# Moving one pair's query preparation from slot 8 to slot 3 of a 16-slot schedule

## Chip, core and metric

One Trainium2 chip, one core used, everything in float32 (some tiles in its rounded matmul form, some small ones in bf16). The metric is device time of one call in microseconds, median of the runs shown. The engines are PE (matmul), DVE (VectorE), ACT (ScalarE), POOL (GpSimd) and SP (SyncE, which here only issues DMAs).

## What is computed

Three layers over x (32 batches of 64 tokens, 256 wide), cut to what matters here:

```python
x = x + xattn(layernorm(x), ctx)     # 16 heads of 16; ctx is (32, 1601, 256)
#   q = qdq(x) @ qdq(wq).T + bq;  k, v = split(ctx @ wkv.T + bkv)
#   o = softmax(q k^T / 4) v;     out = qdq(o) @ qdq(wp).T + bp
x = x + scan(layernorm(x))           # x_proj, softplus(dt), selective scan over 64 tokens
x = x + moe(layernorm(x))            # 64 experts, top 8, capacity 2*2048*8/64
```

`qdq` divides a row by its largest absolute value over 127, rounds, clips and multiplies back. The change touches only where the queries q are made and how the values v are dealt over time. All of it lies in the first phase, which does attention, scan and routing; expert and combine phases follow it.

## The kernel before

**Pairs, slots and strips.** Two batches (128 tokens) are a pair, i; there are 16. A pair has 16 slots, one for each strip of scores: batch b (strips 0 to 7 are b=0, 8 to 15 are b=1), half g of the heads, two heads s. Step G is pair G // 16, slot G % 16. All engines walk over G, each with its own hand-written order and semaphores between them; an engine never passes a waiting instruction.

In step G, PE does in this order: scores of strip G (`scores`, 12 matmuls into the one score area S, four PSUM banks), the turning of the probabilities of strip G-1 (13 transposes in four jobs `turn(G, 0..3)`, called T0 to T3 below), one unit of the values of a batch (`v_mm`), the products of earlier probabilities with values (`times_v`), and the keys of strip G+4 (`k_mm`). Small jobs of the rest of the layers stand in between as `MIX` says: (slot, place) to names. Scores of G wait for the exponential of G-1, which reads S.

DVE takes the row maximum of S (`strip_max`), copies values out (`v_up`), does the mixer's elementwise work (`rest_a`, `rest_b`, `rest_c`, `scan_unit`, `sum_unit`), makes the low part of the keys (`k_low`), and then what stands at the slot's end. ACT does the exponential (`soft`), the copies of the four turned jobs (`turned`), the high part of the keys (`k_up`).

**The ring.** T, V, K jobs and all small ones write into a ring of three PSUM banks W, by the job's number mod 3 in the list that `jobs_at` makes. A job waits on PE (`take`) until the job three before it has been copied out: by ACT if that was a T job, by DVE for every other.

```python
    if G % SLOTS in NO_VALUES:
        return turns + small_at(G, 0) + keys + small_at(G, 1)
    return turns[:2] + small_at(G, 0) + v + turns[2:] + small_at(G, 1) + keys + small_at(G, 2)
```

In a slot of `NO_VALUES` there is no V job; all four T jobs come first. There ACT's order is T0, T1, T2, exponential, T3, keys' high part; elsewhere it is T0, T1, exponential, T2, T3, keys.

**The queries.** For pair i+1 the kernel loads its x (SP, L430), then on DVE `moments_q` (L889 to L891), `norm_q` (L933, L872 to L874) and `round_q` (L883 to L885), each at the end of one slot behind `k_low`; then PE turns the result (job XQ, L579), DVE copies it (`x_up`, L943), PE multiplies with wq (job Q, L588), DVE adds the bias (`q_out`, L951). POOL takes the reciprocal root between `moments_q` and `norm_q` (L485) and parts the queries into high and low (`part_q`, L495 to L499); SP deals them to the four row groups (L398) in slot 12 for b=0 and slot 0 of the next pair for b=1.

**The values.** A batch has 13 tiles of keys in seven units: six of two tiles, and unit 5, the last tile alone (68 keys). Units are made in the order 0 to 6, one a slot.

The mixer of a pair runs behind it: its steps m are slot 4 of the next pair (m=0) to slot 3 of the one after (m=15). In slots 0 to 3 of pair i it is pair i-2 that is finished (scan's last unit in slot 0, third norm in 1, logits in 2, top 8 and places in 3). In slots 4 to 8 it is pair i-1 (quantised attention output, projection, second norm, x_proj, dt).

Of the kernel before, what the change touches and what calls it, by code (L numbers as in the profile page):

```python
# [20 lines left out]
PAIRS = TOK // P  # L21
# [13 lines left out]
V_UNITS = [[2 * u, 2 * u + 1] for u in range(KT // 2 - 1)] + [[KT - 1], [KT - 3, KT - 2]]  # L35
BANKS = 3
WIDTHS = [4, 3, 3, 3]
NO_VALUES = (0, 8)
ALL_STRIPS = PAIRS * SLOTS
CLEARS = 2 * SLOTS  # L40
Y_CLEARS = 16
# [12 lines left out]
END = SLOTS * (PAIRS + 1) + LAG  # L54

MIX = {(4, 0): ["O3"], (5, 0): ["oqT"], (5, 1): ["proj"], (6, 0): ["ln2T"], (6, 1): ["xp"], (7, 0): ["dt"],
       (8, 0): ["XQ"], (8, 1): ["Q"], (10, 0): ["O0"], (14, 0): ["O1"], (1, 0): ["yT"],
       (2, 0): ["O2", "ln3T"], (2, 1): ["logits"], (3, 2): ["pos"]}

QS = NS // 4  # L60
UNITS = 2 * NS // QS
# [24 lines left out]
def values_at(G):  # L86

    i, slot = divmod(G, SLOTS)
    if 1 <= slot <= 7 and i < PAIRS:
        return i, 1, slot - 1  # L90
    if slot >= 9 and i + 1 < PAIRS:
        return i + 1, 0, slot - 9
    return None
# [115 lines left out]
def mixer_phase(nc, io, dram):  # L209
    with ExitStack() as ctx:  # L210
# [78 lines left out]
        ln3T = oqT  # L289
# [86 lines left out]
        def _(sp):  # L376
# [39 lines left out]
            for G in range(END):  # L416
                i, slot = divmod(G, SLOTS)
                cur, nxt = i < PAIRS, i + 1 < PAIRS
                p, m = mixer_at(G)
                if slot == 0 and cur:  # L420
                    deal_queries(i, 1)
                if slot == 12 and nxt:
                    deal_queries(i + 1, 0)
                if G < CLEARS:
                    clear(G)
                elif G < CLEARS + Y_CLEARS:
                    clear_y(G - CLEARS)
                if slot == 0 and nxt:
                    sp.wait_ge(ring_full, full_at("XQ", i))
                    sp.dma_start(x_q[:], x_rows(i + 1)).then_inc(x_in, 16)  # L430
                if slot == 3 and 1 <= i <= PAIRS:
                    after(sp, dve_up, dve_at(i - 2, "X2"))
                    sp.dma_start(x_res[:], x_rows(i - 1)).then_inc(xr_in, 16)
                if nxt and slot in (4, 11):
                    sp.wait_ge(ring_full, full_at("K", G + STRIPS - (1 if slot == 4 else 0)))
                    load_ctx(i + 1, slot // 8)
                if m == 2 and p is not None:
                    sp.wait_ge(ring_free["dve"], free_at("xp", p))
                    sp.dma_start(dram["bc"], BCT[:]).then_inc(bc_out, 16)

                    sp.wait_ge(bc_out, 16 * (p + 1))
                    for part, landed in enumerate((b_in, c_in)):
                        own = slice(part * NS, (part + 1) * NS)
                        sp.dma_start(BC[:, own, :].rearrange("p n t -> p (n t)"),
                                     dram["bc"][own, :].rearrange("n t -> (n t)").partition_broadcast(P)).then_inc(landed, 16)
                if m == 13 and p is not None:
                    sp.wait_ge(dve_up, dve_at(p, "LN3"))
                    sp.dma_start(dram["x3"][bass.ds(p * P, P), :], x3[:]).then_inc(x3_out, 16)
# [6 lines left out]
        def _(pool):  # L455
# [72 lines left out]

            for i in range(PAIRS + 2):
                ended, prev, nxt = i >= 2, 1 <= i <= PAIRS, i + 1 < PAIRS  # L530
                if ended:
                    pool.wait_ge(dve_up, dve_at(i - 2, "V3"))
                    pool.tensor_tensor(st[:, 17:18], st[:, 16:17], neg_half[:], ALU.pow).then_inc(pool_up, 1)  # L533
                if nxt:
                    rstd_q(i + 1)
                if prev:
                    pool.wait_ge(dve_up, dve_at(i - 1, "V2"))
                    pool.tensor_tensor(st[:, 9:10], st[:, 8:9], neg_half[:], ALU.pow).then_inc(pool_up, 1)  # L538
                if prev:
                    for unit in range(UNITS // 2):  # L540
                        scan_input(i - 1, unit)
                if nxt:
                    part_q(i + 1)
                for part in range(4):
                    if ended and i != PAIRS:
                        scatter(i - 2, part)
                    if prev:
                        scan_input(i - 1, UNITS // 2 + part)
                if i == PAIRS:
                    for part in range(4):  # L550
                        scatter(i - 2, part)
# [317 lines left out]
        def _(dve):  # L869
# [303 lines left out]
            for G in range(END):  # L1173
# [8 lines left out]
                for job in small_at(G, 0):  # L1182
                    if job[0] == "O":
                        norm_o(job[1])
                if slot == 8 and nxt:
                    x_up(i + 1)
                if mix and m < 15:
                    rest_a(p, m, link)
# [13 lines left out]
                    route_link = route_begin(i - 2)  # L1202
                if G + STRIPS < ALL_STRIPS:
                    k_low(G + STRIPS)
                if slot == 8 and nxt:
                    q_out(i + 1)
                if mix:
                    if m - FIRST_DECAY - 1 in SUMMED_LATE:
                        sum_unit(p, m - FIRST_DECAY - 1, link)
                    rest_c(p, m, link)  # L1210
                if slot == 1 and nxt:
                    q_link = moments_q(i + 1)
                if slot == 2 and nxt:
                    norm_q(i + 1, q_link)
                if slot == 4 and nxt:
                    round_q(q_link)
                if mix and m == 15:
                    link.end()
# [398 lines left out]
```

## Time and profile before

| | |
|---|---|
| median of 3 runs | 2306.09 us (2305.89 to 2307.5) |
| profiled execution | 2303.75 us, span 2302.0 us |
| PE busy | 2101.8 us (91%) |
| DVE busy | 1752.8 us (76%) |
| ACT busy | 1444.5 us (63%) |
| POOL busy | 677.5 us (29%) |

PE's ends are modelled and its matmuls are pipelined, so rows on PE can overlap and its share says little about free time. The start of a row is what to go by. The 256 steps of the first phase reach from about 34 us to 1770 us. A step is best measured from the first score matmul of one strip to that of the next.

### The profile page before, as it was taken

What the parts mean: (1) busy time and instruction counts of PE and PEld (TensorE: products, weight loads), DVE (VectorE), ACT (ScalarE), POOL (GpSimd) and SP (SyncE); (2) the same over time, 40 slices, a digit from 0 to 9 for tenths busy, and PEclk for the clock granted to TensorE, in tenths of its full rate; (3) what the DMA queues carried; (4) which work ended last, traced back from release to release, by engine and by line L of the source; (5) the groups of instructions that cost most, each with busy time, mean ns of one, the idle gap of its engine ahead of it and who ended that gap; (6) DMA issues with size and microseconds to landing.
All of it is one profiled execution on the core that took longest, in us unless ns stands there. A gap on an engine that the chain in (4) does not pass through costs nothing. (4 is left out here: it accounts for less than half of the span.)

```text
span 2302.0 us, 56038 instructions
## 1 busy us (share of the span) xinstructions
PE 2101.8 (91%) x21448; PEld 1454.3 (63%) x21448; DVE 1752.8 (76%) x3728; ACT 1444.5 (63%) x3012; POOL 677.5 (29%) x646
## 2 busy tenths in 40 slices
PE   7999999999999999999999999999997149999975
PEld 5666666666666666666666666666665037777754
DVE  5557887979797878888888888887978736656646
ACT  2667676868676767676767767676767124445433
POOL 1002040404031322213130404040403437777770
PEclk9999999999999999999999999999999569999998
DMA  7585662323131313232323233232320136676648
GB/s 225 195 283 208 235 256 70 113 81 89 72 88 72 93 67 93 74 86 77 88 84 101 88 72 105 55 105 56 109 51 32 54 119 211 198 232 209 202 137 329
DMA packets 132711, 294.16 MB, mean 128 GB/s; under 512 B 21899, under 2 KB 89143, under 8 KB 126304
## 3 DMA queue, kind: packets, MB, share of 16 engines
q1 hardware_dynamic: 114016, 255.89, 35.2%
q0 software_dynamic: 18432, 34.69, 4.3%
q8 instruction: 174, 2.85, 0.5%
q14 instruction: 89, 0.73, 0.1%
HBM read 165.40 MB, written 108.27 MB: 119 GB/s over the span
## 5 line engine op out<-in xcount | busy, mean ns | idle before, releaser
L799 ACT ACTIVATE sb_probs<-S,sb_negmax 128x1604 f32<-128x1604 f32 x256 | 409.4, 1599 | 246.7 <-DVE sb_negmax L977 246.3
L791 ACT ACTIVATE sb_probsT<-W 128x384 f32<-128x384 f32 (+1 forms) x1024 | 473.9, 513 | 66.3 <-PE W L637 63.6
L637 PE MATMUL W<-sb_ident,sb_probs 128*128 128x128 f32 (+1 forms) x3328 | 484.1, 280 | 23.3 <-DVE sb_o_tok L990 11.9
L977 DVE TENSOR_REDUCE sb_negmax<-S 128x1 f32<-128x1604 f32 x256 | 465.8, 1820 | 2.4 <-PE S L627 1.2
L637 PEld LDWEIGHTS W<-sb_ident,sb_probs 128*128 128x128 f32 (+1 forms) x3328 | 363.0, 139 | 148.4 <-issue 68.5
L610 PE MATMUL W<-sb_wkv_in,sb_ctx 128*128 128x256 f32 (+1 forms) x1664 | 409.0, 388 | 14.9 <-ACT sb_probsT L791 7.2
L600 PE MATMUL W<-sb_ctx,sb_wkv_in 128*32 128x401 f32 x4096 | 399.5, 504 | 4.9 <-DVE sb_V L971 2.5
L610 PEld LDWEIGHTS W<-sb_wkv_in,sb_ctx 128*128 128x128 f32 (+1 forms) x1664 | 292.0, 186 | 76.9 <-ACT sb_probsT L791 26.2
L1330 POOL DMA_INDIRECT y_scratch<-sb_ys,sb_places x256 | 264.0, 1031 | 111.3 <-issue 104.8
L961 DVE SCALAR_TENSOR_TENSOR sb_K_lo<-W,sb_pair_cols,sb_K_hi 128x401 fp32r<-128x401 f32 x256 | 162.0, 633 | 171.5 <-ACT sb_K_hi L783 171.3
L783 ACT ACTIVATE sb_K_hi<-W,sb_pair_cols 128x401 fp32r<-128x401 f32 x256 | 153.2, 598 | 218.2 <-PE W L600 218.2
L510 POOL TENSOR_TENSOR sb_bx<-sb_u,sb_BC 128x512 f32<-128x512 f32 x128 | 165.1, 1306 | 349.1 <-DVE sb_u L1105 219.8
L655 PE MATMUL O<-sb_probsT,sb_V 128*32 128x128 f32 (+1 forms) x6656 | 243.9, 276 | 0.0
L600 PEld LDWEIGHTS W<-sb_ctx,sb_wkv_in 128*32 128x32 f32 x4096 | 130.3, 110 | 118.6 <-issue 104.0
L655 PEld LDWEIGHTS O<-sb_probsT,sb_V 128*32 128x32 f32 (+1 forms) x6656 | 173.2, 109 | 47.8 <-issue 35.2
L971 DVE COPY sb_V<-W 128x512 f32<-128x512 f32 (+1 forms) x224 | 145.4, 649 | 30.2 <-PE W L610 28.5
L522 POOL DMA_INDIRECT xe_scratch<-sb_row,sb_sc_idx x128 | 149.8, 1170 | 43.8 <-issue 30.8
L627 PEld LDWEIGHTS S<-sb_K_hi,sb_Q_hi 32*128 32x128 f32 x1024 | 49.7, 181 | 159.9 <-issue 157.4
L538 POOL TENSOR_TENSOR sb_st<-sb_st,sb_neg_half 128x1 f32<-128x1 f32 x16 | 8.8, 549 | 428.5 <-DVE sb_st L1086 428.5
L1451 DVE TENSOR_TENSOR sb_hid<-U,sb_sg 96x512 f32<-96x512 f32 x64 | 44.0, 687 | 113.5 <-PE U L1359 113.0
L533 POOL TENSOR_TENSOR sb_st<-sb_st,sb_neg_half 128x1 f32<-128x1 f32 x16 | 9.1, 568 | 397.0 <-DVE sb_st L891 397.0
L627 PE MATMUL S<-sb_K_hi,sb_Q_hi 32*128 32x400 f32 (+1 forms) x1024 | 116.5, 444 | 9.9 <-ACT sb_probs L799 7.7
(188 smaller groups left out, 2918.7 us busy)
## 6 DMA issues: line engine op xcount, KB each, us to landing
sb_ctx<-ctxT SPq DMA_DIRECT2D x32, 1604.0 KB, 7.6
xe_scratch<-sb_none SPq DMA_DIRECT2D x32, 1088.0 KB, 13.4
sb_xg<-xe_scratch SPq DMA_DIRECT2D x64, 544.0 KB, 4.2
sb_BC<-bc_scratch SPq DMA_DIRECT2D x32, 1024.0 KB, 6.0
sb_Q_hi<-sb_q_hi SPq DMA_DIRECT2D x128, 128.0 KB, 4.5
sb_Q_lo<-sb_q_lo SPq DMA_DIRECT2D x128, 128.0 KB, 5.4
y_scratch<-sb_none SPq DMA_DIRECT2D x16, 1024.0 KB, 11.3
sb_rows<-y_scratch SPq DMA_DIRECT2D x16, 1024.0 KB, 8.6
```

Source lines behind the costliest of these rows:

```text
L510: pool.tensor_tensor(bx[:, mine, :], u[:, h, :].unsqueeze(1).to_broadcast([P, QS, P]), BC[:, mine, :], ALU.mult).then_inc(pool_up, 1)
L600: ins = pe.matmul(W[32 * c:32 * c + 32, 0:CK], wkv_in[:, k, w0:w0 + 32], ctx_t[b][:, k, c * CK:(c + 1) * CK], start=(k == 0), stop=(k == D ...
L610: ins = pe.matmul(W[0:keys_in(t), n * D:(n + 1) * D], ctx_t[b][:, k, t * P:t * P + keys_in(t)], wkv_in[:, k, D:2 * D], start=(k == 0), sto ...
L627: ins = pe.matmul(S[:, 512 * c:512 * c + cn], q[half][rows, s, g, :, :].rearrange("p h n -> p (h n)"), k[rows, s, 0:cn], start=(n == 0), s ...
L637: ins = pe.transpose(W[0:keys_in(t), at * P:(at + 1) * P], probs[n % 2][:, t * P:t * P + keys_in(t)], ident[:])
L655: ins = pe.matmul(O[32 * s:32 * s + 32, 0:P], V[b][0:keys_in(t), t, g * P + 32 * s:g * P + 32 * s + 32], probsT[k][n % (k + 1)][0:keys_in( ...
L783: act.activation(K_hi[:, s, 0:CK], ring[bank_of("K", n)][:, 0:CK], ACT.Identity, bias=pair_cols[:, g * STRIPS + s:g * STRIPS + s + 1]).the ...
L791: act.activation(probsT[k][n % (k + 1)][:, 0:wide], ring[bank_of("T", G, k)][:, 0:wide], ACT.Copy)\
L799: act.activation(probs[n % 2][:].rearrange("p (c k) -> p c k", c=QUADS), scores_of, ACT.Exp, bias=negmax[:, slot:slot + 1], accum_out=den[ ...
L961: dve.scalar_tensor_tensor(K_lo[:, s, 0:CK], bank("K", n)[:, 0:CK], pair_cols[:, g * STRIPS + s:g * STRIPS + s + 1], K_hi[:, s, 0:CK].bitc ...
L977: dve.tensor_reduce(negmax[:, slot:slot + 1], scores_of, AX.XY, ALU.max, negate=True).then_inc(max_done, 1)
L1330: pool.indirect_dma_start(dram["y"], bass.IndirectOffsetOnAxis(ap=places[e % 4][:, c:c + 1], axis=0), ys[n][:, c, :], None, bounds_check=T ...
```

## The change

Pair i+1's turned, projected and parted queries move five slots up, to slot 3. The three DVE stages ahead of them move with them: moments to slot 0, norm to slot 1, rounding to slot 2. Slot 3 has no values now, and slot 8 has. So the units 0 to 6 of b=1 are made in slots 1, 2, 4, 5, 6, 7, 8 (before: 1 to 7): unit 5, of 68 keys, moves from slot 6 to slot 7. The load of x for pair i+2 is issued behind slot 8's place in SP's order, for pair 1 at step 0. On POOL the parting stands ahead of the second norm's root in place of behind the first four scan inputs.

```diff
-NO_VALUES = (0, 8)
+NO_VALUES = (0, 3)
...
-       (8, 0): ["XQ"], (8, 1): ["Q"], (10, 0): ["O0"], (14, 0): ["O1"], (1, 0): ["yT"],
-       (2, 0): ["O2", "ln3T"], (2, 1): ["logits"], (3, 2): ["pos"]}
+       (3, 0): ["XQ"], (3, 1): ["Q", "pos"], (10, 0): ["O0"], (14, 0): ["O1"], (1, 0): ["yT"],
+       (2, 0): ["O2", "ln3T"], (2, 1): ["logits"]}
...
-    if 1 <= slot <= 7 and i < PAIRS:
-        return i, 1, slot - 1
+    if 1 <= slot <= 8 and slot not in NO_VALUES and i < PAIRS:
+        return i, 1, slot - 1 - (slot > NO_VALUES[1])
...
-                if slot == 0 and nxt:
-                    sp.wait_ge(ring_full, full_at("XQ", i))
-                    sp.dma_start(x_q[:], x_rows(i + 1)).then_inc(x_in, 16)
+                if G == 0 or (slot == 8 and i + 2 < PAIRS):
+                    pair = i + 1 if G == 0 else i + 2
+                    sp.wait_ge(ring_full, full_at("XQ", pair - 1))
+                    sp.dma_start(x_q[:], x_rows(pair)).then_inc(x_in, 16)
...
             for i in range(PAIRS + 2):
                 ended, prev, nxt = i >= 2, 1 <= i <= PAIRS, i + 1 < PAIRS
+                if nxt:
+                    rstd_q(i + 1)
                 if ended:
                     pool.wait_ge(dve_up, dve_at(i - 2, "V3"))
                     pool.tensor_tensor(st[:, 17:18], st[:, 16:17], neg_half[:], ALU.pow).then_inc(pool_up, 1)
                 if nxt:
-                    rstd_q(i + 1)
+                    part_q(i + 1)
                 if prev:
                     pool.wait_ge(dve_up, dve_at(i - 1, "V2"))
                     pool.tensor_tensor(st[:, 9:10], st[:, 8:9], neg_half[:], ALU.pow).then_inc(pool_up, 1)
                 if prev:
                     for unit in range(UNITS // 2):
                         scan_input(i - 1, unit)
-                if nxt:
-                    part_q(i + 1)
...
-                if slot == 8 and nxt:
+                if slot == 3 and nxt:
                     x_up(i + 1)
...
-                if slot == 8 and nxt:
+                if slot == 3 and nxt:
                     q_out(i + 1)
...
+                if slot == 0 and nxt:
+                    q_link = moments_q(i + 1)
                 if slot == 1 and nxt:
-                    q_link = moments_q(i + 1)
+                    norm_q(i + 1, q_link)
                 if slot == 2 and nxt:
-                    norm_q(i + 1, q_link)
-                if slot == 4 and nxt:
                     round_q(q_link)
```

What stands where, at three places. First DVE from the end of slot 0 to the row maximum of slot 2, in a pair from 2 to 14 (`sb_K_lo` is `k_low`, `sb_negmax<-S` is `strip_max`, `sb_st<-sb_x_q` the moments of the next pair's x); before:

```order
L961 SCALAR_TENSOR_TENSOR sb_K_lo<-W,sb_pair_cols,sb_K_hi 128x401
L977 TENSOR_REDUCE sb_negmax<-S 128x1
L1053 TENSOR_TENSOR sb_x<-W,sb_x 128x256
...
L971 COPY sb_V<-W 128x512
L1109 TENSOR_SCALAR sb_row<-sb_x,sb_st 128x256
L961 SCALAR_TENSOR_TENSOR sb_K_lo<-W,sb_pair_cols,sb_K_hi 128x401
L889 BN_STATS sb_st<-sb_x_q 128x6
L203 MEMSET sb_pause_q 128x1
L890 BN_AGGR sb_st<-sb_st 128x2
L891 TENSOR_SCALAR sb_st<-sb_st 128x1
L977 TENSOR_REDUCE sb_negmax<-S 128x1
```

And with the change, where line numbers behind L430 are one higher:

```order
L962 SCALAR_TENSOR_TENSOR sb_K_lo<-W,sb_pair_cols,sb_K_hi 128x401
L890 BN_STATS sb_st<-sb_x_q 128x6
L203 MEMSET sb_pause_q 128x1
L891 BN_AGGR sb_st<-sb_st 128x2
L892 TENSOR_SCALAR sb_st<-sb_st 128x1
L978 TENSOR_REDUCE sb_negmax<-S 128x1
...
L962 SCALAR_TENSOR_TENSOR sb_K_lo<-W,sb_pair_cols,sb_K_hi 128x401
L934 TENSOR_SCALAR sb_x_q<-sb_x_q,sb_st 128x256
L873 TENSOR_REDUCE sb_st<-sb_x_q 128x1
L874 TENSOR_SCALAR sb_st<-sb_st 128x1
L875 RECIPROCAL sb_st<-sb_st 128x1
L978 TENSOR_REDUCE sb_negmax<-S 128x1
```

The moments stand ahead of slot 1's row maximum in place of slot 2's, and ahead of slot 2's stands the norm with its scale.

Second, PE in slot 3 behind its scores (`sb_probs` are the T jobs, L610 the values, L655 the products with values, L600 the keys, `sb_sel` the job pos); before:

```order
L637 MATMUL W<-sb_ident,sb_probs 128x128 x7
L610 MATMUL W<-sb_wkv_in,sb_ctx 128x256 x4
L637 MATMUL W<-sb_ident,sb_probs 128x128 x5
L637 MATMUL W<-sb_ident,sb_probs 68x128
L655 MATMUL O<-sb_probsT,sb_V 32x128 x12
L600 MATMUL W<-sb_ctx,sb_wkv_in 32x401 x8
L715 MATMUL W<-sb_sel,sb_before 128x64
L716 MATMUL W<-sb_sel,sb_ones 128x64
```

And with the change:

```order
L638 MATMUL W<-sb_ident,sb_probs 128x128 x12
L638 MATMUL W<-sb_ident,sb_probs 68x128
L656 MATMUL O<-sb_probsT,sb_V 32x128 x12
L580 MATMUL W<-sb_ident,sb_x_q 128x128 x2
L601 MATMUL W<-sb_ctx,sb_wkv_in 32x401 x8
L589 MATMUL W<-sb_xqT,sb_wqT 128x128 x4
L716 MATMUL W<-sb_sel,sb_before 128x64
L717 MATMUL W<-sb_sel,sb_ones 128x64
```

The values have gone and the four T jobs stand together. XQ is ahead of the keys and Q behind them, which puts Q three jobs behind T3, on its bank.

Third, DVE at the end of slot 4, up to the row maximum of slot 5; before:

```order
L885 TENSOR_SCALAR sb_o_tok<-sb_o_tok,sb_st 128x256
L961 SCALAR_TENSOR_TENSOR sb_K_lo<-W,sb_pair_cols,sb_K_hi 128x401
L883 TENSOR_SCALAR sb_x_q<-sb_x_q,sb_st 128x256
L884 TENSOR_SCALAR sb_x_q<-sb_x_q 128x256
L885 TENSOR_SCALAR sb_x_q<-sb_x_q,sb_st 128x256
L977 TENSOR_REDUCE sb_negmax<-S 128x1
```

And the same place with the change:

```order
L886 TENSOR_SCALAR sb_o_tok<-sb_o_tok,sb_st 128x256
L962 SCALAR_TENSOR_TENSOR sb_K_lo<-W,sb_pair_cols,sb_K_hi 128x401
L978 TENSOR_REDUCE sb_negmax<-S 128x1
```

The three rounding instructions on the next pair's x have left this place; they stand at the end of slot 2 now.

## Rows read from the trace of the kernel before

**Rows 1.** Page: busy time of each engine, share, instructions

```profile
PE 2101.8 (91%) x21448; PEld 1454.3 (63%) x21448; DVE 1752.8 (76%) x3728; ACT 1444.5 (63%) x3012; POOL 677.5 (29%) x646
```

**Rows 2.** PE's timeline, pair 8, slots 1 to 3: start us, us, engine, line, operation

```profile
912.12 1.55 PE L600 MATMUL W<-sb_ctx,sb_wkv_in 128*32 128x401 f32 x16
913.60 0.45 PE L627 MATMUL S<-sb_K_hi,sb_Q_hi 32*128 32x402 f32 x4
...
921.90 0.45 PE L627 MATMUL S<-sb_K_hi,sb_Q_hi 32*128 32x402 f32 x4
...
928.58 0.19 PE L715 MATMUL W<-sb_sel,sb_before 128*128 128x64 bf16 x1
...
928.73 0.46 PE L627 MATMUL S<-sb_K_hi,sb_Q_hi 32*128 32x402 f32 x4
```

**Rows 3.** DVE's timeline, pair 8, slots 1 to 3

```profile
911.37 0.69 DVE L971 COPY sb_V<-W 128x512 f32<-128x512 f32 x1
...
914.92 0.42 DVE L889 BATCH_NORM_STATS2 sb_st<-sb_x_q 128x6 f32<-128x256 f32 x1
...
915.66 1.82 DVE L977 TENSOR_REDUCE sb_negmax<-S 128x1 f32<-128x1604 f32 x1
...
923.22 0.40 DVE L933 TENSOR_SCALAR sb_x_q<-sb_x_q,sb_st 128x256 f32<-128x256 f32 x1
...
924.50 1.83 DVE L977 TENSOR_REDUCE sb_negmax<-S 128x1 f32<-128x1604 f32 x1
```

**Rows 4.** PE's timeline, last pair: first scores of slots 2, 3, 5, 6

```profile
1683.86 0.45 PE L627 MATMUL S<-sb_K_hi,sb_Q_hi 32*128 32x402 f32 x4
...
1691.63 0.46 PE L627 MATMUL S<-sb_K_hi,sb_Q_hi 32*128 32x402 f32 x4
...
1705.02 0.46 PE L627 MATMUL S<-sb_K_hi,sb_Q_hi 32*128 32x402 f32 x4
...
1712.94 0.45 PE L627 MATMUL S<-sb_K_hi,sb_Q_hi 32*128 32x402 f32 x4
```

**Rows 5.** Timelines of PE and DVE, pair 8, slots 4 to 6

```profile
930.83 2.00 PE L610 MATMUL W<-sb_wkv_in,sb_ctx 128*128 128x256 f32 x8
...
935.77 0.45 PE L627 MATMUL S<-sb_K_hi,sb_Q_hi 32*128 32x402 f32 x4
...
944.55 0.45 PE L627 MATMUL S<-sb_K_hi,sb_Q_hi 32*128 32x402 f32 x4
...
938.08 1.82 DVE L977 TENSOR_REDUCE sb_negmax<-S 128x1 f32<-128x1604 f32 x1
```

**Rows 6.** Timelines of ACT and PE, pair 8, slot 8 and start of slot 9

```profile
961.59 1.60 ACT L799 ACTIVATE sb_probs<-S,sb_negmax 128x1604 f32<-128x1604 f32 x1
...
963.16 0.50 ACT L791 ACTIVATE sb_probsT<-W 128x384 f32<-128x384 f32 x1
...
963.76 1.16 PE L588 MATMUL W<-sb_xqT,sb_wqT 128*128 128x128 f32 x8
964.85 0.46 PE L627 MATMUL S<-sb_K_hi,sb_Q_hi 32*128 32x402 f32 x4
```

**Rows 7.** Timelines of PE and DVE, pair 8, slots 6 and 7

```profile
946.43 1.08 PE L610 MATMUL W<-sb_wkv_in,sb_ctx 128*68 128x256 f32 x4
...
948.46 0.66 PE L691 MATMUL W<-sb_ln2T,sb_xpT 128*128 128x128 f32 x4
...
959.10 0.63 DVE L961 SCALAR_TENSOR_TENSOR sb_K_lo<-W,sb_pair_cols,sb_K_hi 128x401 fp32r<-128x401 f32 x1
```

**Rows 8.** DVE's timeline, pair 8, slot 8

```profile
962.96 1.20 DVE L1138 TENSOR_SCALAR sb_topf<-sb_topf 128x8 f32<-128x8 f32 x1
```

**Rows 9.** Pair 0: SP's issue, its time to landing (DMA view), DVE in slot 1

```profile
35.92 0.48 SPq L430 DMA_DIRECT2D sb_x_q<-x  x1
...
sb_x_q<-x SPq DMA_DIRECT2D x1, 128.0 KB, 7.2
...
40.09 1.82 DVE L977 TENSOR_REDUCE sb_negmax<-S 128x1 f32<-128x1604 f32 x1
```

## The prediction

> **What bounds the kernel now.** I read the page first: PE is busy for 91% of the span, DVE for 76% [rows 1]. PE's share says little, since its ends are modelled, so I went to PE's timeline and measured each step from the first score matmul of one strip to that of the next. Over pairs 2 to 14 the steps of one slot number agree to a few hundredths, so one pair (8, steps 128 to 143) stands for all thirteen. Its slots differ, though each turns, multiplies and makes keys alike: slot 2 takes 913.60 to 921.90 = 8.30 us, slot 3 takes 6.83 [rows 2], slot 5 takes 8.78 [rows 5]. The excess is partly small matmuls and partly PE standing before a ring bank that DVE has not yet copied out. Next I read DVE's timeline: in each slot it takes the row maximum first and only then the copies that free banks, so whatever stands between `k_low` and that maximum makes every copy of the next slot late. This is how the query work costs time though DVE has idle time elsewhere.
>
> The trace has its own experiment on this. The last pair has no next pair, hence no moments, norm or rounding. Its slot 2 takes 1691.63 - 1683.86 = 7.77 against 8.30, its slot 5 takes 1712.94 - 1705.02 = 7.92 against 8.78 [rows 4, 2, 5]. So the moments ahead of slot 2's maximum cost 0.53 and the rounding ahead of slot 5's costs 0.86.
>
> **The change, part by part, for one of pairs 2 to 14.**
>
> *Slot 1: moments move ahead of its maximum.* They take 915.66 - 914.92 = 0.74 from their start to that of the maximum [rows 3]. Everything behind it on DVE slides by 0.74: the add of the third residual, its moments, then the values' copy, which ends at 911.37 + 0.69 = 912.06 [rows 3]. The keys of that slot take the bank of the values and start at 912.12 [rows 2], 0.06 after: there is no slack. **+0.74.** (If PE had been held there by its own queue as well, it could be as little as 0.5.)
>
> *Slot 2: norm and scale in place of the moments ahead of its maximum.* 924.50 - 923.22 = 1.28 against 0.74 [rows 3], 0.54 more. The 0.74 there now costs 0.53 by the last pair, so what slack there was is used up and the rest counts in full: **+0.54**.
>
> *Slot 3: values go, XQ and Q come.* Rounding stands ahead of its maximum as it does now in slot 5, where the maximum starts 938.08 - 935.77 = 2.31 after the slot's first scores [rows 5]. It takes 1.83 [rows 3], so the exponential starts at 4.14. Without values ACT copies T3 only behind the exponential, and Q takes T3's bank. In slot 8 now the exponential starts at 961.59, T3's copy is over at 963.16 + 0.50 = 963.66, Q starts at 963.76, and the next scores at 964.85 [rows 6]: 2.17 and 1.09. Q in slot 3 then starts at 4.14 + 2.17 = 6.31, and with the job pos, 928.73 - 928.58 = 0.15 [rows 2], the next scores at 6.31 + 1.09 + 0.15 = 7.55, against 6.83 now. **+0.72.** That is the point of this forecast: in slot 8 nothing stands ahead of the maximum, in slot 3 the rounding does. From below: if Q waited for the keys alone, PE's own work would decide, which loses values of 2.00 [rows 5] and gains Q's 1.09 [rows 6] and the two transposes of XQ, estimated at half of that: -0.4.
> XQ, `x_up` and the top 8 chain of that slot lie on DVE beside the exponential and T3's copy, which hide them; without that cover pos would come later by what they overhang. DVE's `q_out` and the two place additions follow `k_low`, as the place additions do now, so slot 4's maximum starts about as long after its scores as now. So 0 for slot 4.
>
> *Slot 5: nothing ahead of its maximum.* **-0.86**, by the last pair [rows 4]. It can't be more: there nothing is left ahead of it.
>
> *Slot 6: two tiles of values in place of the last one.* Values now start at 946.43 and take 1.08, and x_proj starts at 948.46 in their bank [rows 7]. Two tiles take 2.00 [rows 5] and their copy 0.69 [rows 3]: 946.43 + 2.00 + 0.69, with some 0.1 between, is 949.22 to 949.25. **+0.78.**
>
> *Slots 7 and 8.* The short unit is in slot 7 now, but DVE does not profit: its softplus chain ends where it did, since it hangs on the exponential, and `k_low` runs 959.10 to 959.73 [rows 7]. Slot 8's values take the bank of these keys, so they start at 959.78, and from values to next scores it is 935.77 - 930.83 = 4.94 in slot 4, which has as many products [rows 5]. That gives 964.72 for the start of slot 9 against 964.85 [rows 6]. **-0.13.** The two ends: 0.6 more if the late values make a late `k_low`, 0.5 less if the chain gets shorter.
>
> *Sum for a pair:* 0.74 + 0.54 + 0.72 - 0.86 + 0.78 - 0.13 = 1.79, times 13 = 23.3 us.
>
> *The other pairs.* Pair 0: x of pair 1 is issued at 35.92 and lands 7.2 later, at 43.1; the moments now want it at 40.09, where slot 1's maximum starts [rows 9]. DVE waits 3.0, and with the moments that maximum is 3.8 late. Pair 0 has no mixer work to squeeze, so I take 2.6 of it (2 to 3.8). Its slot 3 adds 0.7. Pair 1 has slots 2, 3, 5 to 8 as above, slot 1 nearly free: 1.1. The last pair has values missing in slot 3 and added in slot 8, which cancel, and slot 6: about 0.9. Together 5.3.
>
> *POOL and SP* cost nothing here: POOL's next work behind the parting is the second norm's root, for which it waits until slot 5 is nearly over, a whole slot after the parting. If the parting ran into it, slot 6 would start late by the overhang. The load of x now goes out ahead of the next context's and is wanted only in the next pair's slot 0. The scatters come earlier by the parting's length, and nothing waits for them.
>
> Sum: 23.3 + 5.3 = 28.6 on the profiled 2303.75 us, which is 2332. The median of the runs is 2.3 above the profiled one, so I predict **2335 us**, 1.25% slower.
>
> **Rivals.**
>
> *Faster: the ring doesn't bind.* If PE were held by its own work alone in slots 1 to 3 and 6 to 8, moving matmuls from slot to slot would cancel and the 0.86 of slot 5 would be left, on 14 pairs -12 us: 2294. For it: PE's 91%, and that no instruction is added. Against it: 912.06 and 912.12 in slot 1, 963.66 and 963.76 in slot 8. It decides where the waits of slots 1, 2, 3 and 6 come to less than the 1.0 that slots 5, 7 and 8 give back; I make them 2.8. Chance 0.10.
>
> *No change:* the waits come to just about that, 2301 to 2310.7. 0.06.
>
> *Q in slot 3 goes as in slot 8.* The gate on T3 isn't what holds Q; slot 3 gets -0.4 in place of +0.72, 15 pairs, -17: 2318. 0.14.
>
> *POOL's parting blocks DVE in slot 4.* In slot 8 a DVE instruction on 8 columns takes 1.20 us [rows 8]; it lies under POOL's scan input and ends with it. The parting now lies in slot 4, where DVE quantises the attention output for slot 5. One such block of about 1 us on 14 pairs would give 2349. Against it: the parting starts right with slot 4, the quantising only behind the maximum and the values' copy, over 4 us into the slot by my estimate (maximum 1.0 in, 1.82 long [rows 3], then two copies). The Trainium skill ("SBUF — State Buffer", section "Who interferes with whom") says that VectorE and GpSimd lock a shared port pair and that the second to issue blocks until the first is done; it names two-input operations and `tensor_scalar`, of which the quantising is made. By that rule every overlap would cost, but a row maximum, which fills the first half of slot 4, would not. 0.12.
>
> The forecast itself has 0.58, with its own range 2322 to 2346. To hold 8 in 10 the range takes in the last two rivals but not the first two: **2313 to 2351**. A measurement of this kernel tells some 0.2% (4.6 us) from no change; faster 0.10, same 0.06, slower 0.84.
>
> **What would show it.** Measured between first scores, in pair 8: slot 1 longer by 0.7, with the keys right behind the values' copy; slot 2 8.8; slot 3 7.5, with Q right behind ACT's copy of T3; slot 5 7.9; slot 6 longer by 0.8; slots 7 and 8 together as now. In pair 0 a DVE wait of about 3 us on the x load. The prediction is wrong if slot 3 is under 6.9 or if slots 1 and 2 are unchanged.

## The result, and the profile after

The changed kernel takes 2328.52 us, median of 4 runs (2326.57 to 2329.66), against 2306.8 (2305.89 to 2309.68): a ratio of 1.0093 [1.0078, 1.0108], so it is slower by 0.9%. A second timing later, 10 runs against 13 of before, gives 1.0089 [1.0066, 1.0112]. The forecast was 2335, slower, with a range of 2313 to 2351.

First the page of the changed kernel, to be held against [rows 1]:

```profile
PE 2104.4 (90%) x21448; PEld 1459.4 (63%) x21448; DVE 1753.7 (75%) x3728; ACT 1444.1 (62%) x3012; POOL 657.7 (28%) x646
```

PE is busy 2.6 us longer than before and DVE 0.9, ACT and POOL less, while the span is 26 us longer (2327.9 against 2302.0). So this is waiting in the main, not work. From the first scores of step 0 to those of step 255 it is 1731.64 us before and 1755.03 after, +23.4. What lies outside that is 570.4 us of the span before and 572.9 after, where the change leaves every engine's order as it was.

To say in which slot, I measure again from first scores to first scores. This is PE's timeline of the changed kernel in pair 8: slots 1 to 3, the first scores of slots 6 and 7, and the values of slot 8, for [rows 2, 5 to 7] (columns: start us, us, engine, line, operation, output and inputs, count):

```profile
920.95 0.45 PE L628 MATMUL S<-sb_K_hi,sb_Q_hi 32*128 32x402 f32 x4
...
927.10 1.55 PE L601 MATMUL W<-sb_ctx,sb_wkv_in 128*32 128x401 f32 x16
928.58 0.46 PE L628 MATMUL S<-sb_K_hi,sb_Q_hi 32*128 32x402 f32 x4
...
937.43 0.45 PE L628 MATMUL S<-sb_K_hi,sb_Q_hi 32*128 32x402 f32 x4
...
943.71 1.16 PE L589 MATMUL W<-sb_xqT,sb_wqT 128*128 128x128 f32 x8 [1.16 <-ACT sb_probsT L792]
944.70 0.19 PE L716 MATMUL W<-sb_sel,sb_before 128*128 128x64 bf16 x1
944.85 0.46 PE L628 MATMUL S<-sb_K_hi,sb_Q_hi 32*128 32x402 f32 x4
...
959.80 0.46 PE L628 MATMUL S<-sb_K_hi,sb_Q_hi 32*128 32x402 f32 x4
...
967.66 0.46 PE L628 MATMUL S<-sb_K_hi,sb_Q_hi 32*128 32x402 f32 x4
...
975.77 1.96 PE L611 MATMUL W<-sb_wkv_in,sb_ctx 128*128 128x256 f32 x8
```

Slot 1 is 920.95 to 928.58, slot 2 from there to 937.43, and so on. The table has the slots of pair 8 that differ, in us. The other eight agree to 0.02, save slot 4 with 7.03 to 7.08. "Best" is the changed kernel with the three repairs at the end of the experiments. The columns from "stages alone" on are experiments below.

| slot | before | after | stages alone | T3 early in slot 3 | short unit in slot 6 | stages ahead of `k_low`, before | same, after | best |
|---|---|---|---|---|---|---|---|---|
| 1 | 6.89 | 7.63 | 7.63 | 7.63 | 7.63 | 6.89 | 6.89 | 6.89 |
| 2 | 8.30 | 8.85 | 8.84 | 8.85 | 8.84 | 7.77 | 7.77 | 7.77 |
| 3 | 6.83 | 7.43 | 6.53 | 6.26 | 7.43 | 6.36 | 6.45 | 6.20 |
| 5 | 8.78 | 7.92 | 7.92 | 7.92 | 7.92 | 7.91 | 7.92 | 7.91 |
| 6 | 7.05 | 7.86 | 7.05 | 7.86 | 7.05 | 7.05 | 7.86 | 7.05 |
| 7 | 6.72 | 6.55 | 6.72 | 6.54 | 6.72 | 6.72 | 6.55 | 6.72 |
| 8 | 6.53 | 6.47 | 6.52 | 6.47 | 6.41 | 6.52 | 6.47 | 6.41 |
| 9 | 6.48 | 6.31 | 6.48 | 6.31 | 6.31 | 6.49 | 6.32 | 6.31 |
| pair | 110.03 | 111.47 | 110.15 | 110.33 | 110.77 | 108.17 | 108.67 | 107.72 |
| step 0 to 255 | 1731.6 | 1755.0 | 1736.0 | 1737.6 | 1744.5 | 1707.6 | 1714.1 | 1699.7 |

DVE's timeline of the changed kernel in the same stretch, for [rows 3]:

```profile
922.67 0.41 DVE L890 BATCH_NORM_STATS2 sb_st<-sb_x_q 128x6 f32<-128x256 f32 x1
923.41 1.82 DVE L978 TENSOR_REDUCE sb_negmax<-S 128x1 f32<-128x1604 f32 x1
...
926.35 0.69 DVE L972 COPY sb_V<-W 128x512 f32<-128x512 f32 x1
...
929.90 0.40 DVE L934 TENSOR_SCALAR sb_x_q<-sb_x_q,sb_st 128x256 f32<-128x256 f32 x1
...
931.18 1.83 DVE L978 TENSOR_REDUCE sb_negmax<-S 128x1 f32<-128x1604 f32 x1
...
938.75 0.34 DVE L884 TENSOR_SCALAR sb_x_q<-sb_x_q,sb_st 128x256 f32<-128x256 f32 x1
...
939.73 1.82 DVE L978 TENSOR_REDUCE sb_negmax<-S 128x1 f32<-128x1604 f32 x1
...
963.72 0.69 DVE L972 COPY sb_V<-W 128x512 f32<-128x512 f32 x1 [0.44 <-PE W L611]
...
975.05 0.63 DVE L962 SCALAR_TENSOR_TENSOR sb_K_lo<-W,sb_pair_cols,sb_K_hi 128x401 fp32r<-128x401 f32 x1
```

Read it as pairs of rows. In slot 1 the moments start 0.74 ahead of the maximum, the values' copy ends at 926.35 + 0.69 = 927.04, and the keys, in that bank, start at 927.10: the same 0.06 as before, 0.74 later in the slot. In slot 2 the norm starts 1.28 ahead of the maximum. In slot 6 the copy ends at 964.41 and x_proj, in that bank, starts at 964.46. The low part of slot 7's keys ends at 975.05 + 0.63 = 975.68 and slot 8's values start at 975.77. Slot 3's row maximum starts 939.73 - 937.43 = 2.30 after the slot's scores, where it was 2.31 in slot 5 before. What follows from it on ACT:

```profile
941.59 1.60 ACT L800 ACTIVATE sb_probs<-S,sb_negmax 128x1604 f32<-128x1604 f32 x1 [1.41 <-DVE sb_negmax L978]
943.17 0.48 ACT L792 ACTIVATE sb_probsT<-W 128x384 f32<-128x384 f32 x1
```

The exponential starts at 4.16 into the slot, T3 is copied behind it until 943.65, and Q starts at 943.71, for which PE had stood 1.16 us.

### The profile page after: what moved, and what is told of

Read it like the earlier page. It is cut to its first block and busy times, and to the rows that moved or that the text cites. A ratio compares the mean times of both kernels' runs of the same rounds, so it can differ in the third digit from the quotient of the medians.

```text
span 2327.9 us, 56038 instructions
## 1 busy us (share of the span) xinstructions
PE 2104.4 (90%) x21448; PEld 1459.4 (63%) x21448; DVE 1753.7 (75%) x3728; ACT 1444.1 (62%) x3012; POOL 657.7 (28%) x646
## 5 line engine op out<-in xcount | busy, mean ns | idle before, releaser
L611 PEld LDWEIGHTS W<-sb_wkv_in,sb_ctx 128*128 128x128 f32 (+1 forms) x1664 | 293.8, 186 | 79.0 <-ACT sb_probsT L792 28.6
L523 POOL DMA_INDIRECT xe_scratch<-sb_row,sb_sc_idx x128 | 137.5, 1074 | 43.7 <-issue 30.8
L486 POOL TENSOR_TENSOR sb_st<-sb_st,sb_neg_half 128x1 f32<-128x1 f32 x16 | 9.0, 564 | 421.6 <-DVE sb_st L892 421.6
L1371 PE MATMUL Y<-sb_wd,sb_hid 96*128 96x256 f32 x512 | 123.0, 383 | 3.7 <-DVE sb_ys L1445 3.7
```

What stands on the lines that cost most here:

```text
L611: ins = pe.matmul(W[0:keys_in(t), n * D:(n + 1) * D], ctx_t[b][:, k, t * P:t * P + keys_in(t)], wkv_in[:, k, D:2 * D], start=(k == 0), sto ...
```

## Experiments

In all of these the theory is the forecast's: a stage between `k_low` and the row maximum makes every copy of the next slot late, and the banks of the ring turn that into PE's waiting. Slot times come from one profiled execution and agree from pair to pair within a few hundredths, except that on the chip where before takes 2391.98 a few pairs are 0.1 to 0.4 longer than the others; the numbers given are those of most pairs.

**The stages alone.** The stages on x move to the ends of slots 0, 1 and 2 in the kernel before; XQ, Q, the values and the parting stay where they were. As in the change, x is loaded a pair ahead and POOL's root of it comes first; the cut shows DVE's part.

```diff
-                if slot == 1 and nxt:
+                if slot == 0 and nxt:
                     q_link = moments_q(i + 1)
-                if slot == 2 and nxt:
+                if slot == 1 and nxt:
                     norm_q(i + 1, q_link)
-                if slot == 4 and nxt:
+                if slot == 2 and nxt:
                     round_q(q_link)
```

> The kernel before with one part of the change: moments, norm and rounding of the next pair's x at the ends of slots 0, 1, 2 (x loaded a pair ahead, POOL's root of it first); the matmuls XQ and Q, the values and the parting stay as before. My theory (whatever stands ahead of a row maximum on DVE makes the bank copies behind it late): a pair's slot 1 takes 7.63 as in the changed kernel (6.89 before), slot 2 8.84 (8.30), slot 3 about 6.55 (6.84), slot 5 7.92 (8.78), all others as before, slot 9 at 6.48 among them; a pair about 110.2 us against 110.03 before, and pair 0 some 3 us more for the x load. Rival (moving the matmuls is what costs, DVE's stages are hidden): slots 1 and 2 as before, a pair 109.2 or less.

It took 2313.51 against 2305.22 for one run of before on that chip. Slots 1, 2, 3 and 5 took 7.63, 8.84, 6.53 and 7.92, the pair 110.15: the theory's numbers to 0.05. The 256 steps took 4.3 us more than before, 2.8 of it in pair 0; the rest of the 8.3 lies behind them (541.8 against 536.0), where nothing was changed. Of the change's +1.44 for a pair the stages make only +0.12; +1.32 comes with the matmuls (slot 3 +0.90, slot 6 +0.81, slots 7 to 9 -0.39). The three moved delays nearly cancel, +0.74 +0.54 -0.30 -0.86: slot 3 gains 0.30 although the rounding now stands ahead of its maximum, since the norm with its scale stood there before, 1.28 long, and the rounding takes 939.73 - 938.75 = 0.98 in the rows above. It is the meeting of rounding and Q in slot 3 that costs.

**T3 ahead of the exponential in slot 3.** If the gate on T3 holds Q, ACT's order undoes it:

```diff
                     turned(G, 2)
+                if strip and G % SLOTS == 3:
+                    turned(G, 3)
...
-                if strip:
+                if strip and G % SLOTS != 3:
                     turned(G, 3)
```

> The changed kernel, but in slot 3 ACT copies T3 ahead of the exponential. My theory (Q takes T3's bank and waits for that copy): Q starts right behind the keys, about 5.1 after the slot's first scores in place of 6.28, slot 3 falls from 7.42 to about 6.2, slot 4 grows by 0.2 at most, because keys' copies and the place additions now reach into it; a pair 110.4 in place of 111.47, in all about 2314 us. Rival (Q waits for x_up or PE is full anyway): slot 3 stays above 7.2.

2311.12 (before: 2305.22). Slot 3 took 6.26, the pair 110.33. ACT's and PE's timelines of this kernel in slot 3 show the order and its effect:

```profile
928.12 1.76 ACT L792 ACTIVATE sb_probsT<-W 128x384 f32<-128x384 f32 x4
930.90 1.60 ACT L800 ACTIVATE sb_probs<-S,sb_negmax 128x1604 f32<-128x1604 f32 x1 [1.02 <-DVE sb_negmax L980]
```

```profile
930.31 1.55 PE L601 MATMUL W<-sb_ctx,sb_wkv_in 128*32 128x401 f32 x16
931.79 1.16 PE L589 MATMUL W<-sb_xqT,sb_wqT 128*128 128x128 f32 x8
```

All four copies are over before the exponential begins; Q now starts right behind the keys, with no wait. The rival "Q in slot 3 goes as in slot 8" falls: T3's copy did hold Q, and it cost 1.17 us of slot 3. Slot 4 takes 7.08 in place of 7.03, so hardly any of it is given back: the pair is 1.14 shorter. Against the kernel before, slot 3 is now 0.57 shorter; the forecast's own lower bound for it was -0.4.

**The short unit back in slot 6.** Unit 5 (68 keys) is made in slot 6 again, the two-tile unit in slot 7:

```diff
-        return i, 1, slot - 1 - (slot > NO_VALUES[1])
+        return i, 1, (0, 1, 2, 3, 5, 4, 6)[slot - 1 - (slot > NO_VALUES[1])]
```

> The changed kernel, but the short unit of the values (the last tile alone) is made in slot 6 as before the change, the unit of tiles 8 and 9 in slot 7. My theory: slot 6 falls from 7.86 to 7.05, slots 7 and 8 together rise from 13.02 to 13.1, a pair 110.7 to 110.8. Rival (PE's work is only shifted, so it comes back): slots 6 to 8 together stay at 20.9.

2316.24. Slot 6 took 7.05, as before the change, slots 7 and 8 together 13.13 (13.02 in the changed kernel), the pair 110.77. PE's timeline of this kernel in slot 6:

```profile
955.29 1.08 PE L611 MATMUL W<-sb_wkv_in,sb_ctx 128*68 128x256 f32 x4
...
957.32 0.66 PE L692 MATMUL W<-sb_ln2T,sb_xpT 128*128 128x128 f32 x4
```

The values take 1.08 and x_proj starts 2.03 behind their start. In the changed kernel it waits for two tiles and their copy, 961.69 to 964.46:

```profile
961.69 1.99 PE L611 MATMUL W<-sb_wkv_in,sb_ctx 128*128 128x256 f32 x8
...
964.46 0.71 PE L692 MATMUL W<-sb_ln2T,sb_xpT 128*128 128x128 f32 x4
```

The same tile of extra matmul costs 0.81 in slot 6 and 0.11 in slots 7 and 8: in one place seven times what it costs in the other. Slot 7 is back at 6.72 too, so the 0.17 that it loses in the changed kernel is the short unit's.

**The parting at its old place in POOL's order**, behind the scan inputs, but with the queries already made in slot 3:

```diff
-                if nxt:
-                    part_q(i + 1)
                 if prev:
...
                         scan_input(i - 1, unit)
+                if nxt:
+                    part_q(i + 1)
```

> The changed kernel, but POOL parts the queries behind the first four scan inputs as before. My theory: POOL's work is hidden, all slots as in the changed kernel (slot 4 7.03, slot 9 6.31; the scan of slot 9 on DVE is longer by 0.7 and hidden). Rival (POOL's parting in slot 4 costs, or its going from slot 9 is what made slot 9 shorter): slot 4 shorter, or slot 9 back at 6.48.

2380.97: my theory had it without effect, and **it fell**. Slot 9 takes 10.46 in most pairs. DVE's timeline there, and POOL's beside it:

```profile
1001.24 1.21 DVE L1139 TENSOR_SCALAR sb_topf<-sb_topf 128x8 f32<-128x8 f32 x1
1002.48 0.96 DVE L1140 TENSOR_TENSOR scores_all<-sb_top,sb_topf 128x8 f32<-128x8 f32 x1
1003.47 0.97 DVE L1142 TENSOR_SCALAR sb_row<-sb_topf 128x8 f32<-128x8 f32 x1
1004.48 0.17 DVE L1143 TENSOR_SCALAR sb_row<-sb_tokid 128x8 f32<-128x8 f32 x1
1004.68 1.17 DVE L1144 TENSOR_SCALAR sb_topf<-sb_topf 128x8 f32<-128x8 f32 x1
...
1006.17 0.63 DVE L962 SCALAR_TENSOR_TENSOR sb_K_lo<-W,sb_pair_cols,sb_K_hi 128x401 fp32r<-128x401 f32 x1
```

```profile
1002.37 1.04 POOL L496 TENSOR_TENSOR sb_q_own<-sb_q_f,sb_headmask 128x512 f32<-128x512 f32 x1
1003.37 1.05 POOL L497 TENSOR_TENSOR sb_q_hi<-sb_q_f,sb_headmask 128x512 fp32r<-128x512 f32 x1
1004.56 1.26 POOL L500 TENSOR_TENSOR sb_q_lo<-sb_q_own,sb_q_hi 128x512 fp32r<-128x512 f32 x1
```

Each instruction of the routing works on 8 columns; L1143, issued between two of POOL's, takes 0.17. Three others end when an instruction of the parting does: 1002.48 + 0.96 = 1003.44 beside L496's 1003.41, 1003.47 + 0.97 = 1004.44 beside L497's 1004.42, and 1004.68 + 1.17 = 1005.85 beside L500's 1005.82. These three take 3.10 in place of the 0.51 that the same lines take in the changed kernel. The first row, L1139, is not the parting's doing: it lies under the last scan input and takes 1.20 in the changed kernel as well. The Trainium skill ("SBUF — State Buffer", section "Who interferes with whom") says that where a DVE instruction needs the ports that DVE shares with GpSimd, the second of the two to issue blocks until the first is done; in these rows the second to start is DVE's each time, and they agree. Before the change the parting could not start until slot 8's Q was out; with Q in slot 3 it starts as soon as the scan inputs end, on top of the routing. That makes `k_low` late, and then PE:

```profile
1006.85 2.98 PE L611 MATMUL W<-sb_wkv_in,sb_ctx 128*128 128x256 f32 x8 [2.31 <-DVE sb_K_lo L962]
```

The window view of that stretch, cut fine (columns: stretch, its length, busy time of PE, PEld, DVE, ACT and POOL, then PEclk, the share of TensorE's full clock that was granted, DMA share, GB/s):

```profile
1004.50:1006.80 2.30, 0.04 (x1) 0.00 (x0) 2.20 (x6) 1.21 (x4) 1.46 (x2) 1.00 0.00 0
1006.80:1008.50 1.70, 1.65 (x6) 1.39 (x7) 1.70 (x1) 0.00 (x0) 1.07 (x1) 0.77 0.00 0
1008.50:1010.20 1.70, 1.70 (x7) 1.31 (x6) 0.36 (x2) 1.64 (x2) 0.97 (x1) 0.50 0.22 82
1010.20:1011.90 1.70, 1.70 (x31) 1.36 (x32) 1.61 (x3) 1.12 (x3) 0.00 (x0) 0.73 0.22 82
```

PE stood for 2.3 us, started again at the full clock, and was then granted 0.5 (1.2 of 2.4 GHz): the three windows lose 0.39, 0.85 and 0.46, together 1.7, which is 3.4 us at half. So values that take 1.96 took 2.98. The two parts can be told apart, because not every pair has the fall: slot 9 is 8.77 and the pair 113.9 without it, 10.46 and 115.6 with it. Blocking costs 2.4 us a pair and the clock 1.7 more where it falls.

**The parting behind the routing.** As above, and POOL waits for the routing first:

```diff
+                if nxt:
+                    after(pool, routed, i - 1)
+                    part_q(i + 1)
```

> The changed kernel with POOL's parting behind the first four scan inputs and, in addition, behind the end of the routing of that slot (POOL waits for the indices). In the run with the parting right behind the scan inputs slot 9 took 10.46 in place of 6.31; there seven small DVE instructions of the routing took about 1 us each under POOL's parting. If that collision is the cause, slot 9 is back at 6.3 to 6.5 here, though POOL does the same work in the same slots. If the late parting or what follows it on POOL is the cause, slot 9 stays near 10.

2406.38 on a chip on which before takes 2391.98. Slot 9 took 6.32 and most pairs 111.47, as in the changed kernel, though POOL's parting now lies in slot 9. So it was the overlap with the routing, not the parting's lateness. The expectation counts seven slow instructions; the rows above show three under the parting and one under the last scan input.

**The stages ahead of `k_low` in place of behind it, in the kernel before.** If the delay ahead of the maximum is the cost, then DVE's idle time ahead of `k_low`, where it waits for the keys, should take the same instructions for nothing. Moments go there in slot 1, norm and rounding in slot 2; nothing is left at the slots' ends.

```diff
+                if slot == 1 and nxt:
+                    q_link = moments_q(i + 1)
+                if slot == 2 and nxt:
+                    norm_q(i + 1, q_link)
+                    round_q(q_link)
                 if G + STRIPS < ALL_STRIPS:
...
-                if slot == 1 and nxt:
-                    q_link = moments_q(i + 1)
-                if slot == 2 and nxt:
-                    norm_q(i + 1, q_link)
-                if slot == 4 and nxt:
-                    round_q(q_link)
```

> The kernel before (queries and values where they were), but the DVE stages stand ahead of the keys' low part in place of behind it: moments in slot 1, norm and rounding in slot 2, where DVE idles 1.8 and 2.4 us for ACT. My theory (a stage costs only what it puts ahead of a row maximum): slots 2, 3 and 5 of a pair fall to what the last pair shows, 7.77, 6.36 and 7.92, a pair 108.2 in place of 110.03, in all about 2280 us. Rival (these stages cost wherever they stand, since DVE's time is short): a pair stays within 0.5 of 110.03.

2359.17 against 2391.98, a ratio of 0.986 [0.9836, 0.9884]. Slots 2, 3 and 5 take 7.77, 6.36 and 7.91, the pair 108.17 in place of 110.03. On this chip the four kernels profiled took some 75 us longer behind the 256 steps (613 to 616 in place of 536 to 542), so the first phase is what compares with the other traces: 24.1 us less than before. The median falls by 32.8. The other 9 us can't be given to the edit: the three other kernels on this chip also come out 7 to 9 us better against before than their steps say, the one with the parting behind the routing among them (14.4 us slower in its time, 23.7 in its steps). The kernel before was not profiled on that chip, so why stays open; its ratios there flatter by 0.3 to 0.4%.

**The same on the changed kernel**, and **with the two other repairs** (T3 early in slot 3, short unit in slot 6). POOL's root of the next x goes back behind the third norm's, as before the change; the cut shows DVE's part:

```diff
...
+                if slot == 1 and nxt:
+                    q_link = moments_q(i + 1)
+                if slot == 2 and nxt:
+                    norm_q(i + 1, q_link)
+                    round_q(q_link)
                 if G + STRIPS < ALL_STRIPS:
...
-                if slot == 0 and nxt:
-                    q_link = moments_q(i + 1)
-                if slot == 1 and nxt:
-                    norm_q(i + 1, q_link)
-                if slot == 2 and nxt:
-                    round_q(q_link)
```

> The changed kernel with the same: moments in slot 1, norm and rounding in slot 2, all ahead of the keys' low part. My theory: slot 1 6.89, slot 2 7.77, slot 3 about 6.5 (the exponential starts 0.95 earlier, so T3's copy and Q do), a pair 108.7 in place of 111.47, pair 0 loses its wait for x, in all about 2287 us: still some 0.5 a pair behind the kernel above, by slot 6. Rival (the moved matmuls are what costs): slots 3 and 6 stay at 7.4 and 7.9, in all over 2300.

> The changed kernel with all three: stages ahead of the keys' low part, T3 copied ahead of the exponential in slot 3, the short unit of the values in slot 6. My theory: slot 3 6.2, slot 6 7.05, a pair 107.7, in all about 2274 us, under both kernels and under the kernel before with its stages ahead. Rival (the gains overlap): not under 2285.

2367.22 and 2352.12 against 2391.98: 0.9904 [0.9883, 0.9925] and 0.9834 [0.9814, 0.9855]. The pairs take 108.67 and 107.73. With the stages out of the way slot 3 takes 6.45 although Q still waits for T3, so that gate costs 0.25 now and not 1.17: the maximum comes earlier, the exponential with it, and T3's copy behind it.

**Both timed again, and x one slot earlier.** The changed kernel and the best one ran once more, on a chip on which before takes 2306.59, with a version that issues pair 1's x ahead of the first dealing:

```diff
+            sp.wait_ge(ring_full, full_at("XQ", 0))
+            sp.dma_start(x_q[:], x_rows(1)).then_inc(x_in, 16)
             deal_queries(0, 0)
...
-                if G == 0 or (slot == 8 and i + 2 < PAIRS):
-                    pair = i + 1 if G == 0 else i + 2
+                if slot == 8 and i + 2 < PAIRS:
+                    pair = i + 2
```

> The changed kernel once more, beside the next two on one chip. 1.0 to 1.2% above the kernel before; a pair 111.47 us. Whether pair 0's slot 1 takes 8.8 or about 7.1 hangs on a fall of the granted clock there, which I expect to come again.

> The version with the stages ahead of the keys' low part, T3 first in slot 3 and the short unit in slot 6, once more. A pair 107.73 us, first phase 31 us shorter than before the change, so 1.2 to 1.6% under the kernel before. If the ratio of the first measurement (0.983) held more than the first phase gives, it is nearer 0.987 here.

> The changed kernel, but pair 1's x is issued ahead of the first dealing of queries, about 11 us earlier. My theory (DVE waits 3 us for this x in pair 0 and nowhere else): pair 0's slot 1 falls from 8.80 to what it is without that wait, 7.85 with the fall of the clock or 6.2 without; all pairs behind it as in the changed kernel, 111.47. Rival (the wait is not what holds slot 1, the moments are): above 8.3.

The changed kernel took 2328.72 against 2306.59, 1.0089 [1.0066, 1.0112], a little under the expected 1.0 to 1.2%; the best one 2272.88 (2272.01 to 2273.62), 0.9841 [0.9783, 0.99]. The interval is wide because one of the 13 runs of before took 2328.97; the medians alone give 0.9854. Its pair is 107.72 and its first phase 1699.67, 32.0 less than before, 1.39% of 2306.59. In microseconds it was expected at 2274; by the medians' ratio "nearer 0.987" was close. DVE's timeline of it at the start of slot 3 shows where the gain is:

```profile
904.81 0.41 DVE L936 TENSOR_SCALAR sb_x_q<-sb_x_q,sb_st 128x256 f32<-128x256 f32 x1
...
906.82 0.35 DVE L888 TENSOR_SCALAR sb_x_q<-sb_x_q,sb_st 128x256 f32<-128x256 f32 x1
...
907.78 1.82 DVE L980 TENSOR_REDUCE sb_negmax<-S 128x1 f32<-128x1604 f32 x1
```

Its slot 3 has its first scores at 906.46. Norm and rounding fill 904.81 to 907.17, 1.65 of these 2.36 us ahead of them, and the maximum starts at 1.32 into the slot, not at 2.30.

The early x took 2329.59. In pair 0 slot 1 takes 7.85 in place of the 8.80 of the changed kernel, so the wait for x was worth 0.95. The other 1.7 over the 6.16 of before stayed; the windows of that slot before, with the change, and with x early say what it is:

```profile
39.15:45.32 6.17, 6.16 (x56) 4.60 (x56) 3.06 (x3) 3.78 (x7) 0.00 (x0) 1.00 1.02 411
```

```profile
39.74:48.54 8.80, 8.06 (x55) 5.55 (x55) 3.73 (x7) 3.42 (x7) 0.56 (x1) 0.81 1.01 410
```

```profile
38.47:46.32 7.85, 7.85 (x56) 5.90 (x56) 3.73 (x7) 4.05 (x7) 0.56 (x1) 0.78 1.01 412
```

The granted clock is 1.00 before, and 0.78 of 7.85 with x early, which is 1.73 us lost. So the x wait costs 0.95 here and the moments nothing, and the rest is the clock.

## Why the forecast was right, and where it was off

The direction and the mechanism held: the reading that DVE's stages ahead of a maximum set the next slot's copies, and the ring PE. By the steps of the forecast:

- *Slot 1, +0.74* (own lower end 0.5): +0.74. *Slot 2, +0.54*: +0.55. *Slot 5, -0.86*: -0.86. The last pair, which has no next x, was a true experiment inside the trace, and the stages alone confirm all three.
- *Slot 3, +0.72*: +0.60. The exponential at 4.16 (4.14 forecast) and Q at 6.28 (6.31) were right. The step that was mis-sized is the 1.09 + 0.15 from Q to the next scores: it is 944.85 - 943.71 = 1.14, since pos starts at 944.70 inside the end of Q's row. That is 0.10 of the 0.12. That T3's copy holds Q was argued from slot 8; the early T3 shows it.
- *Slot 4, 0*: 7.04 and 7.03.
- *Slot 6, +0.78*: +0.81; the short unit in slot 6 takes it back to 7.05.
- *Slots 7 and 8, -0.13*: -0.23. The place was right, values right behind slot 7's `k_low` (975.68 and 975.77); that `k_low` would end where it did was wrong by 0.1.
- *Slot 9*, which I did not cost: -0.17. This is the step that was missing. The forecast followed Q to slot 3 and not what its absence does to the slot after it. Before the change the values of slot 9 took Q's bank; DVE's and PE's timelines of the kernel before show `q_out` ending at 966.44 and the values starting at 966.50, 1.65 into the slot:

```profile
965.84 0.60 DVE L951 TENSOR_SCALAR sb_q_f<-W,sb_q_cols 128x128 f32<-128x128 f32 x2
```

```profile
966.50 1.99 PE L610 MATMUL W<-sb_wkv_in,sb_ctx 128*128 128x256 f32 x8
```

  With the change `k_low` is the copy before them; it ends at 982.11, and the values start 982.16 - 980.68 = 1.48 into the slot. The same timelines of the changed kernel:

```profile
981.47 0.64 DVE L962 SCALAR_TENSOR_TENSOR sb_K_lo<-W,sb_pair_cols,sb_K_hi 128x401 fp32r<-128x401 f32 x1
```

```profile
982.16 1.99 PE L611 MATMUL W<-sb_wkv_in,sb_ctx 128*128 128x256 f32 x8
```

  The stages alone, with Q still in slot 8, leave slot 9 at 6.48, and the parting back in slot 9 leaves it at 6.32: it is Q's absence, not the parting's.

- *Sum for a pair, 1.79*: 1.44, times 13 = 18.7 and not 23.3. The 0.35 is slot 3 (0.12), slots 7 and 8 (0.10), slot 9 (0.17), less 0.04 in slots 2 and 6.
- *Pair 0, +3.3*: +3.84 (99.36 to 103.20). Slot 1 is +2.64 against a forecast 2.6, but that is luck: I costed it as a 3 us wait for x of which most is paid. DVE did wait 3.08:

```profile
43.84 0.43 DVE L890 BATCH_NORM_STATS2 sb_st<-sb_x_q 128x6 f32<-128x256 f32 x1 [3.08 <-DMA sb_x_q<-x]
```

  The experiment with x early gives the wait 0.95, and the granted clock the other 1.7. Whether that 1.7 is the change's doing is not shown (below); without it pair 0 is longer by 2.1.
- *Pair 1, +1.1*: 107.37 to 108.54, +1.17.
- *Last pair, +0.9*: -0.2. The forecast let the values missing in slot 3 and added in slot 8 cancel, which they do (6.36 to 5.01 is -1.35, 5.10 to 6.48 is +1.38), and gave slot 6 its +0.8 (7.05 to 7.87). It missed -0.17 in slot 7 and -0.88 in slot 9: before the change slot 9 took 5.91 there, and 5.03 after. DVE's rows say what slot 9 had: its maximum starts 1734.04 - 1731.81 = 2.23 into the slot before the change and 1758.01 - 1756.67 = 1.34 after. Before, slot 8 has no values and is short there, so POOL's scan inputs reach 0.74 into slot 9 and two routing instructions of 1.2 us lie under them in place of one. The second of them, before and after:

```profile
1731.36 1.20 DVE L1139 TENSOR_TENSOR scores_all<-sb_top,sb_topf 128x8 f32<-128x8 f32 x1
```

```profile
1756.25 0.17 DVE L1140 TENSOR_TENSOR scores_all<-sb_top,sb_topf 128x8 f32<-128x8 f32 x1
```

  So the collision that the old place of the parting brought out was in the trace of before already. No run tests this slot by itself.

- Of the 13 pairs 18.7, and 3.84 + 1.17 - 0.2 = 4.8, sum 23.5: the first phase is longer by 23.4. Forecast 28.6. The profiled execution is longer by 25.9, with 2.5 us outside the steps, and the median moved by 21.7: the profiled one was 3.05 below the median of before and 1.14 above that of after. So the forecast's 2335 is 6.5 too high, of which 5.2 are in the steps.

The rivals. *The ring doesn't bind* is out: pair 8 is slower by 1.44, and the early T3 and the short unit each remove a wait of PE and gain. *Q as in slot 8* would have given 2318; slot 3 shows +0.60 and not -0.4. *The parting blocks DVE in slot 4* didn't happen where it was feared: slot 4 is 7.03; in pair 8 the parting is over at 949.17 and the quantising begins with its row maxima at 950.16. The mechanism itself is real, though, as the old place of the parting showed, at 2.4 us a pair, and 4.1 with the fall of the clock. "POOL costs nothing" was right only because the change moved the parting too; my reasoning, that only an overhang into the second norm would matter, would have passed a kernel of 2381 us.

What stays open: why the clock falls in pair 0 of the changed kernel and of every experiment, and not in that of before (below); and the 7 to 9 us by which, on one chip, before is slower against four kernels than the steps say.

## What to carry to other kernels

On an engine with a fixed order, the place of an instruction can cost more than its length: behind the work for which it had to wait anyway it delays what comes next, ahead of that work it fills a wait. The same ten instructions cost 1.86 us a pair at the slots' ends and next to nothing ahead of `k_low`: slots 2, 3 and 5 then take what the last pair takes without them. When a job moves, follow both ends of the ring, the bank that it now waits for and the job that used to wait for it, and look at what its followers on other engines may now run on top of.

## What the runs showed of the hardware

- DVE instructions on 8 columns took 0.96 to 1.21 us beside POOL's 1.04 to 1.26, and 0.17 without it. Each ended within 0.04 us of POOL's, so each paid for the rest of a POOL instruction: the three under the parting took 3.10 in place of 0.51. The row maximum took 1.82 beside the parting in slot 4 as elsewhere.
- The granted clock fell to 0.5 for about 3.4 us in pairs where PE had stood 2.3 us and had begun again at 1.00, and cost 1.7 us each time. The fall came 0.3 to 1.3 us behind PE's new start. It did not follow from the wait alone: with the parting at its old place 4 of 13 pairs took 113.9 and 9 took 115.6, and PE's timeline in one of the four (pair 6) has the same wait with values at their usual length behind it, where they took 2.98 in pair 8:

```profile
777.34 1.99 PE L611 MATMUL W<-sb_wkv_in,sb_ctx 128*128 128x256 f32 x8 [2.32 <-DVE sb_K_lo L962]
```

  In pair 0 PE stands 2.43 us ahead of slot 1's scores in the changed kernel and 2.44 in the one before; it falls behind the first and not behind the second. Since like pairs of one kernel differ too, one trace of before can't tell whether its pair 0 is always spared. These are PE's timelines with x early (the same 2.43) and before; the values behind them take 3.17 and 1.89:

```profile
38.47 0.46 PE L630 MATMUL S<-sb_K_hi,sb_Q_hi 32*128 32x402 f32 x4 [2.43 <-ACT sb_probs L802]
```

```profile
39.16 0.45 PE L627 MATMUL S<-sb_K_hi,sb_Q_hi 32*128 32x402 f32 x4 [2.44 <-ACT sb_probs L799]
```

- The part of the kernel behind the 256 steps took 536 to 542 us in the profiles of two chips and 613 to 616 in those of a third, while the best kernel's 256 steps took 1700.5 there and 1699.7 on another, 0.05 us a pair apart. Kernels are best compared on one chip, or step by step.
